# Row-by-row fetch of one subtile in every group of four tiles, shared by SyncE and ScalarE, in a two-layer graph kernel

## The reference

```python
def _L0_gnn_ref(feat, src, dst, W, attn_l, attn_r, bias):
    z = (feat @ W).reshape(N, HEADS, PER_HEAD)
    el = jnp.einsum('nhp,hp->nh', z, attn_l)
    er = jnp.einsum('nhp,hp->nh', z, attn_r)
    e = jax.nn.leaky_relu(el[src] + er[dst], negative_slope=NEG_SLOPE)
    a = jnp.exp(e - emax[dst])
    msg = z[src] * a[:, :, None]
    agg = jax.ops.segment_sum(msg, dst, num_segments=N)
    out = agg / jnp.maximum(denom, 1e-09)[:, :, None]

def _L1_gnn_ref(node_feats, edge_attrs, edge_feats, ...):
    h = jax.nn.silu(edge_feats @ A1 + b1)
    h = jax.nn.silu(h @ A2 + b2)
    tpw = h @ A3
    ss = s[sender]; vs = v[sender]
    # four products of ss, vs, the edge attributes and tpw, summed per receiver, then W_out

h = jnp.maximum(_layernorm(x, axis=-1), 0.0)
x = x + _L0_gnn_ref(h, src, dst, ...)
h = jnp.maximum(_layernorm(x, axis=-1), 0.0)
x = x + _L1_gnn_ref(h, edge_attr_4, edge_attr_8, ...)
```

## Time and profile before

| | us |
|---|---|
| Median of 3 runs | 4041.5 (4036.51 to 4043.6) |
| The profiled execution | 4049.47 |
| Its span, first to last instruction | 4047.6 |
| Mean granted TensorE clock | 0.758 |

### The profile page before, as it was taken

One profiled execution on the slowest core, in us unless ns is written; L12 is line 12 of the kernel. 1 busy time (PEld: TensorE's weight loads), 2 busy tenths in 40 slices (PEclk: granted clock), 3 DMA queues, 4 the chain that ended last, 5 costly groups with the idle time before them and its releaser, 6 DMA issues.

```text
span 4047.6 us, 71477 instructions
## 1 busy us (share of the span) xinstructions
PE 3048.9 (75%) x15640; PEld 2582.1 (64%) x15641; DVE 1948.5 (48%) x4563; ACT 1119.0 (28%) x1869; POOL 2961.1 (73%) x3121
## 2 busy tenths in 40 slices
PE   2566666666667656766659989888899898899898
PEld 2556665566667555665647767666677676676676
DVE  7434434333433433434345555555555555555554
ACT  2334434333433434333331111111111111111111
POOL 1777777777777777777747777777777777777775
PEclk9666666666655665666669888888988989988888
DMA  3434343443434343444422222222222222222221
GB/s 107 119 108 119 111 121 109 124 114 108 119 109 118 112 121 104 124 113 114 118 52 59 59 62 61 60 61 60 59 60 61 61 60 61 60 60 61 60 62 49
DMA packets 208656, 352.07 MB, mean 87 GB/s; under 512 B 99631, under 2 KB 129638, under 8 KB 208326
## 3 DMA queue, kind: packets, MB, share of 16 engines
q0 software_dynamic: 99328, 216.34, 21.3%
q1 hardware_dynamic: 108548, 130.56, 10.4%
q10 hardware_dynamic: 450, 2.44, 0.2%
HBM read 338.22 MB, written 10.85 MB: 86 GB/s over the span
## 4 chain that ended last, share of the span: by engine, by line
POOL 66%; issue 24%; DVE 2%; DMA 2%; PE 2%; POOLq 1%; DVEq 1%; SPq 1%; ACT 1%; ACTq 0%
POOL rows L534 66%; DMA rows<-z_tab,idx 1%; DMA rows<-up_tab,idx 1%; POOLq L280 1%; PE pair L1175 0%; SPq L333 0%; ACT L633 0%; POOLq L281 0%; DVE share L1036 0%; PE pair L1307 0%; DMA win_dram<-share 0%; DVE share L1128 0%; PE pair L1264 0%; DVEq L965 0%; PE pair L1270 0%
## 5 line engine op out<-in xcount | busy, mean ns | idle before, releaser
L534 POOL DMA_INDIRECT rows<-z_tab,idx x1552 | 1477.2, 952 | 554.6 <-issue 546.1
L534 POOL DMA_INDIRECT rows<-up_tab,idx x1552 | 1468.0, 946 | 510.3 <-issue 505.4
L1211 PE MATMUL pair<-acc 128*128 x3168 | 572.1, 327 | 443.3 <-ACT acc L621 441.0
L1211 PEld LDWEIGHTS pair<-acc 128*128 128x128 f32 x3168 | 555.3, 272 | 490.4 <-issue 490.4
L1307 PE MATMUL pair<-share 128*128 128x144 f32 x3136 | 833.8, 354 | 0.0
L1305 PEld LDWEIGHTS pair<-share 128*128 128x128 f32 x3136 | 577.1, 217 | 395.6 <-DVE share L1131 220.4
L1243 PE MATMUL pair<-share,acc 128*128 128x136 f32 x3136 | 676.6, 400 | 0.3
L1305 PE MATMUL pair<-share 128*128 128x48 f32 x3136 | 573.1, 268 | 101.3 <-DVE share L1131 101.1
L1243 PEld LDWEIGHTS pair<-share,acc 128*128 128x128 f32 x3136 | 639.2, 299 | 0.5 <-issue 0.4
L1128 DVE TENSOR_TENSOR share<-rows,pair 128x384 f32<-128x384 f32 x784 | 396.6, 547 | 412.7 <-DMA rows<-up_tab,idx 397.6
L1307 PEld LDWEIGHTS pair<-share 128*128 128x128 f32 x3136 | 544.7, 217 | 0.0
(11 more groups left out here) (172 smaller groups left out, 1890.2 us busy)
## 6 DMA issues: line engine op xcount, KB each, us to landing
acc<-dst_tab SPq DMA_DIRECT2D x198, 512.0 KB
lent<-z_tab SPq DMA_DIRECT2D x2060, 0.6 KB
lent<-up_tab SPq DMA_DIRECT2D x2060, 0.5 KB
rows<-z_tab,idx POOLq DMA_INDIRECT x1552
rows<-up_tab,idx POOLq DMA_INDIRECT x1552
ef_sb<-in_edge_f SPq DMA_DIRECT2D x198, 32.0 KB
z_tab<-rows SPq DMA_DIRECT2D x7, 504.0 KB, 3.2
y_sb<-in_edge_y SPq DMA_DIRECT2D x198, 16.0 KB
```

The lines of the kernel that those rows point to most:

```text
L534: pool.indirect_dma_start(out=rows[:, s, t, 0:width], out_offset=None, in_=table, in_offset=bass.IndirectOffsetOnAxis(ap=indices[:, t:t + ...
L1211: mm = t.matmul(bank[6 + h][:, i * 16:i * 16 + 16], hotT[:, h, i * P:(i + 1) * P], er_flat[:, bass.ds(at, 1), :].rearrange("p a f -> p (a ...
```

## The change

**Fetch.** The eighth subtile of the fourth tile is now taken from POOL in every group, not in every third. Its 128 rows are split: SP fetches 80 rows, 20 in each tile, and ACT fetches 48, 12 in each tile. The buffer `lent` becomes two, used in turn, with semaphores of their own for SP's and ACT's rows. SP reads a list of 128 offsets once per group. ACT fetches its parts 2 and 3 of this group's buffer in tiles 0 and 1, and parts 0 and 1 of the next group's in tiles 2 and 3; SP fetches parts 1 to 3 of this group's buffer in tiles 0 to 2, and part 0 of the next one's in tile 3. ACT copies the buffer in the third tile of every group. POOL issues 31 gathers in every group: 1519 per layer.

**Loops.** SP's and ACT's loop bodies hold two groups (`pairs`) where they held three; POOL's and DVE's hold one.

**Blocks.** DVE centres the block and copies the transposed block out of PSUM itself; ACT only takes the square root (`std_block`). SP stores a group's finished blocks one group later than before.

The diff, cut to its core:

```diff
-PER = 3
-LENT = GI // PER
-PARTS = (12,) * 8 + (8,) * 4
+SP_PARTS = (20, 20, 20, 20)
+ACT_PARTS = (12, 12, 12, 12)
+SP_ROWS, ACT_ROWS = sum(SP_PARTS), sum(ACT_PARTS)
...
-        lent = sb("lent", [P, ZW])
-        lent_idx = sb("lent_idx", [1, 2 * P], I32)
+        lent = sb("lent", [P, 2, ZW])
+        lent_idx = sb("lent_idx", [1, 2, P], I32)
...
-        def thirds(eng, body):
-            with eng.Fori(0, LENT) as r:
-                for e in range(PER):
-                    body(r, e)
-            for e in range(GI % PER):
-                body(LENT, e)
+        def pairs(eng, body):
+            with eng.Fori(0, GI // 2) as i:
+                for e in range(2):
+                    body(i * 2 + e, i, e)
+            body(GI - 1, GI // 2, 0)
+
+        def fetch(eng, kind, landed, first, sizes, i, buf, table, width):
+            at, size = first + sum(sizes[:i]), sizes[i]
+            _, offsets = nc.values_load_multi_w_load_instructions(
+                lent_idx[0:1, buf, at:at + size], engines=(kind,), min_val=0, max_val=(NODES - 1) * width,
...
+            for j, offset in enumerate(offsets):
+                eng.dma_start(lent[at + j:at + j + 1, buf, 0:width // 4].bitcast(U8),
+                              table[bass.ds(offset, width)].rearrange("(a b) -> a b", a=1)).then_inc(landed[buf], 16)
...
+            def first_rows(s_l, n, k, table, width):
+                hold(sp, s_l["copied"], k * GI + 1)
                 load_list(s_l, n, 0, 0)
+                hold(sp, s_l["list"], k * (16 * GI) + 16)
+                sp_rows(s_l, 0, 0, table, width)
+
+            def rows_ahead(s_l, n, k, q, e, s, table, width):
+                last = isinstance(q, int)
+                if s == 1 and not last:
+                    hold(sp, s_l["copied"], k * GI + q + 1)
+                    load_list(s_l, n, q + 1, 1 - e)
+                if s < U - 1:
+                    sp_rows(s_l, s + 1, e, table, width)
+                elif not last:
+                    hold(sp, s_l["list"], (k * GI + q) * 16 + 32)
+                    sp_rows(s_l, 0, 1 - e, table, width)
...
                         load_targets(s, q * U + (s + AHEAD))
+                        rows_ahead(s_l1, 0, k, q, e, s, z_bytes, 4 * ZW)
                         if s == 2:
-                            blocks(sp, q + 1, store_up)
-                        fetch_ahead(s_l1, 0, k, r, e, s, z_bytes, 4 * ZW)
+                            blocks(sp, q, store_up)
...
-                            gather(s, idx[:, s, :], tab, width, s_l["rows"][s],
-                                   T - 1 if e == PER - 1 and s == U - 1 else T)
+                            gather(s, idx[:, s, :], tab, width, s_l["rows"][s], T - 1 if s == U - 1 else T)
...
+            def rows_ahead(s_l, k, q, e, s, table, width):
+                if s < 2:
+                    act_rows(s_l, s + 2, e, table, width)
+                elif not isinstance(q, int):
+                    if s == 2:
+                        hold(act, s_l["list"], (k * GI + q) * 16 + 32)
+                        hold(act, s_l["copied"], k * GI + q + 1)
+                    act_rows(s_l, s - 2, 1 - e, table, width)
...
-                nc.scalar.activation(rows[:, U - 1, T - 1, 0:width], lent[:, 0:width], ACT.Copy)\
+                act.wait_ge(s_l["sp_rows"][e], before * (16 * SP_ROWS) + 16 * SP_ROWS)
+                act.wait_ge(s_l["act_rows"][e], before * (16 * ACT_ROWS) + 16 * ACT_ROWS)
+                nc.scalar.activation(rows[:, U - 1, T - 1, 0:width], lent[:, e, 0:width], ACT.Copy)\
...
-                v.tensor_scalar(nmr1, mv1[:, 0:1], -1.0, None, ALU.mult).then_inc(s_mid["mean"], 1)
-                dve.wait_ge(s_mid["norm"], b + 1)
+                v.tensor_scalar(hc_sb, xs, mv1[:, 0:1], 0.0, ALU.subtract, ALU.max).then_inc(s_mid["centred"], 1)
+                dve.wait_ge(s_mid["turned"], b + 1)
+                v.tensor_copy(hcT_sb, bank[0][:, 0:P]).then_inc(s_mid["turned_sb"], 1)
+                dve.wait_ge(s_mid["std"], b + 1)
```

More of the change, by code:

```diff
@@ L49 @@
 LW = ZW + HEADS
[L50 to L56 removed]
+SP_PARTS = (20, 20, 20, 20)
+ACT_PARTS = (12, 12, 12, 12)
+SP_ROWS, ACT_ROWS = sum(SP_PARTS), sum(ACT_PARTS)
+assert SP_ROWS + ACT_ROWS == P and len(SP_PARTS) == len(ACT_PARTS) == U and GI < P and GI % 2 == 1
 assert NB == BU * BI and NG == U * GI and NG * GE >= EDGES and PAD_DST >= NODES + 3 * P and WIN + HALF - 1 <= P
@@ L256, in gnn_kernel @@
         s_in = named("in", node_steps)
-        s_mid = named("mid", ("mean", "centred", "norm", "turned", "turned_sb", "lin", "row", "stored"))
+        s_mid = named("mid", ("mean", "centred", "std", "turned", "turned_sb", "lin", "row", "stored"))
         s_out = named("out", ("agg_staged", "agg", "added", "stored"))
         def edge_sems(tag, names):
-            return named(tag, ("added", "open", "list", "landed", "copied") + names) \
-                | {n: sems(f"{tag}_{n}_slot", U) for n in ("rows", "in")}
+            return named(tag, ("added", "open", "list", "copied") + names) \
+                | {n: sems(f"{tag}_{n}_slot", U) for n in ("rows", "in")} \
+                | {n: sems(f"{tag}_{n}_buf", 2) for n in ("sp_rows", "act_rows")}
         idx_set = sem("idx_set")
@@ L296, in last_blocks, with rows_landed @@
                 work(b)
[L298 to L302, removed]
-        def thirds(eng, body):
-            with eng.Fori(0, LENT) as r:
-                for e in range(PER):
-                    body(r, e)
-            for e in range(GI % PER):
-                body(LENT, e)
+        def rows_landed(s, q):
+            return q * (16 * (T - 1)) + 16 * (T - 1) if s == U - 1 else q * (16 * T) + 16 * T
+        def pairs(eng, body):
[7 more added lines that the diff above has]
+                lent_idx[0:1, buf, at:at + size], engines=(kind,), min_val=0, max_val=(NODES - 1) * width,
+                skip_runtime_bounds_check_because="they are byte offsets of source nodes, which are rows of the table")
+            for j, offset in enumerate(offsets):
+                eng.dma_start(lent[at + j:at + j + 1, buf, 0:width // 4].bitcast(U8),
+                              table[bass.ds(offset, width)].rearrange("(a b) -> a b", a=1)).then_inc(landed[buf], 16)
+        z_bytes = z_tab.rearrange("n f -> (n f)").bitcast(U8)
+        up_bytes = up_tab.rearrange("n f -> (n f)").bitcast(U8)
         IN1 = 16 * (NG + AHEAD) // 2
@@ L409, in store_up @@
                   .then_inc(s_mid["stored"], 16)
[L411 to L442, removed]
@@ L444, in fetch_first, with sp_rows, load_list @@
-            def fetch_first(s_l, n, k, table, width):
-                load_list(s_l, n, 0, 0)
-                hold(sp, s_l["list"], k * (16 * (LENT + 1)) + 16)
-                hold(sp, s_l["copied"], k * LENT + 1)
-                fetch(s_l, 0, 0, table, width)
+            def sp_rows(s_l, i, buf, table, width):
+                fetch(sp, mybir.EngineType.SP, s_l["sp_rows"], 0, SP_PARTS, i, buf, table, width)
+            def load_list(s_l, n, r, buf):
+                sp.dma_start(lent_idx[0:1, buf, :], lent_dram[n:n + 1, bass.ds(r * P, P)]).then_inc(s_l["list"], 16)
```

116 lines of the change are left out of this document (55 added, 61 removed).

## The result

| | us | ratio to before |
|---|---|---|
| Before, median of 4 runs on the same chip | 4039.15 (4036.51 to 4043.6) | |
| Changed, median of 4 runs | 4211.81 (4206.13 to 4219.21) | 1.0425, 95% interval 1.0407 to 1.0443 |
| Its profiled execution, and its span | 4206.13, 4204.3 | |

What follows compares the result with a forecast made beforehand. POOL's gathers bound the kernel before; SP was to take over at 40.25 and 42.3 us per group, ending layer 2 167 us later: 4049.5 + 167 = 4217 profiled, less 8 gives 4209 us; own range 4110 to 4330, overall 3955 to 4330.

Steps and rivals of the forecast that it cites:

- POOL sets the pace before; 31 gathers are 38.8 us: Both layers: before, each lasts as long as POOL's 1552 gathers; afterwards 31 at 1.251 us make 38.8 us per group.
- SP's sum: SP's rows, register loads, stores, list and loop return: 40.25 us per group in layer 1, 42.3 in layer 2.
- The Trainium skill's price for register loads: SP's loads: about 200 ns per register would make 20 values 1.6 us dearer than 12; the trace's line gave 0.45.
- The extrapolation from 8 and 12: SP's register load: 0.692 us for 8 values and 0.919 for 12, extended by line to 1.37 for 20.
- The end of layer 1, 40 us later: Layer 1: SP's last row issued at 2088 against POOL's last gather end at 2048.2, so the layer ends 40 us later.
- The hindrance of the two sequencers: Rival: SP and ACT hinder each other, or ACT binds; rows at 0.368 us, 298 us more, 4507 us; chance 0.13.
- ACT at 35.4 us per group, no bound: ACT with 48 added rows takes about 35.4 us per group, below POOL; binds only if a row costs over 0.4.
- The rival "ACT binds": ACT's added row fetches set the pace if a row costs it over 0.4 us; chance 0.13, shared with sequencers hindering each other.
- Centring on DVE, at nothing, at worst 20 us of cost: Block centring moved to DVE: nothing on the path; with the cover gone at most 49 x 0.4 = 20 us.
- SP keeps up: Rival: POOL still sets the pace and the whole 82.6 us gain comes, 3959 us; chance 0.18.
- How lateness reaches POOL: Third and fourth tiles: ACT's copy waits for SP's last 20 rows, DVE's fourth tile for the copy, POOL for DVE.

Runs made afterwards that it cites:

- f1: Changed kernel with SP fetching 60 rows per group (parts 16, 16, 16, 12), ACT still 48, 20 rows left out: 4135.58 us, 1.0216 of before.
- f3: Changed kernel with SP at 60 rows (16, 16, 16, 12) and ACT at 28 (8, 8, 8, 4), 40 left out: 4033.57 us, 0.9964 of before.
- e2: Changed kernel with ACT fetching 7 rows per tile instead of 12, SP still 80 per group, 20 left out: 4178.0 us, 1.034 of before.
- f2: Changed kernel with ACT fetching 28 rows per group (8, 8, 8, 4), SP still 80, 20 left out: 4178.1 us, 1.0317 of before.
- f4: Changed kernel with ACT again centring the blocks and copying the transposed block, as before the change: 4251.68 us, 1.0505 of before.
- e3: Changed kernel with all 128 rows fetched, 18 per tile on SP and 14 on ACT: 4842.63 us, 1.1994 of before.
- e1: Changed kernel with SP fetching 15 rows per tile instead of 20, ACT still 12, 20 rows left out: 4176.85 us, 1.0332 of before.
- e4: Changed kernel with all 128 rows fetched, 16 per tile on SP and 16 on ACT: 4560.54 us, 1.1305 of before.
- h1: Kernel before plus new scheme in layer 1 alone, four-group loop bodies, SP's stores every second group; slower session: 5889.62 us, 1.0398 of before.

## Why the prediction was right, step by step

- **POOL sets the pace before; 31 gathers are 38.8 us.** Right. Wherever nothing else held layer 1 (f1, f3), the group took 38.9.
- **SP's sum.** Right, and nearly term by term. By SP's own loads the group of layer 1 lasts 39.97 us (40.25 predicted), that of layer 2 42.3 (42.3). Rows follow each other at 0.334 and 0.331 us (0.33), the load of 20 values is 1.39 (1.37), the way back in the loop 2.72 us (2.7). SP's rows ran in layer 2 from 2110.1 to 4176.4, 2066.3 us; the prediction had them from 2128.3 to 4194, 2066. That layer 2 fits so well is in part luck: with ACT relieved SP's group there is 41.9 (e2, f2), so SP's own sum was 0.4 too long, and the chain of ACT and PE gave that back.
- **The Trainium skill's price for register loads.** The row of the trace decided rightly for 20 values: 1.39 us and not 1.6 us more than for 12. The extrapolation from 8 and 12 held because the pieces of 20, like those of 8 and 12, start at multiples of four values; the prediction names no such condition. Where they don't, 7, 14, 15 and 18 values take about 1.7, 3.1, 3.3 and 3.9 us. The Trainium skill (Runtime: NRT & Kernel Launch, Instruction fetch mechanics) puts a register at about 200 ns even in bulk, and these loads agree with it, at 0.20 to 0.25 us per value; those that start at a multiple of four don't, with 0.057 us for each further value.
- **The end of layer 1, 40 us later.** Too late by 18: SP's first row of layer 2 was issued at 2110.0, not at 2128.3. 48 groups x 0.28 us are 13 of it. The profiled execution was thus 157 us longer than before (4206.1 against 4049.5), not 167. That the median came out within 3 us of 4209 owes something to chance: the 8 us by which the median of before lies under its profiled execution were taken off again, while here the median lies 6 us above it.
- **The hindrance of the two sequencers.** Not seen. Rows on SP cost 0.33 us with ACT fetching 12 rows per tile (changed kernel), and SP's group of layer 1 is 39.9 with 12 rows on ACT and with 7 or 8.
- **ACT at 35.4 us per group, no bound.** This is the term that was wrong, without cost to the number. Its rows cost what was said (0.343 us, load 0.94). What was left out is that ACT's rows stand between two products of PE in layer 2, so that the chain PE, ACT, PE gets longer by each of them. The sum was made for layer 1 alone, and in layer 2 the chain is about 42.1 us (f1), as long as SP's. In layer 1 f4 shows that little was left as well. The prediction came out right since SP's 42.3 lay on top of both. The rival "ACT binds" was given its chance on the price of a row, which was fine; its real ground, the place of the rows between PE's products, wasn't named, and a forecast by the prediction's own sum (the full 38.8 in both layers, 3957 us) was 179 us wrong for f1 and 77 for f3.
- **Centring on DVE, at nothing, at worst 20 us of cost.** Undoing it costs 32 to 40 us (f4), so it was no cost: it keeps ACT under SP in layer 1. How much of that is the work and how much ACT's longer way back isn't shown.
- **SP keeps up.** Fell: SP has no slack left in the trace, and nor would the 3959 us have come if it had kept up (f1, f3).
- **How lateness reaches POOL.** The prediction named ACT's copy of the late rows and DVE's fourth tile. ACT's copy waited for row fetches only 36.2 us in 24 places, and POOL waits most for ACT's indices, 211.6 us. DVE's wait for the copy was there, 90.8 us in layer 1 and 34.4 in layer 2, 1.3 us per group over both, and small beside its 667.9 us for ACT's exponentials. ACT's and SP's programs as a whole run late; the copy is one gate among others.

## What to carry to other kernels

Before work moves onto a sequencer, add up all that it issues per round and compare that with the round of the engine that is relieved; here the sum from five rows of the trace hit the round within 1%, and SP's waits before the change (13.5 us per group in layer 1, 9.2 in layer 2) told at once that 37 more rows at 0.33 us, 12.3 us, wouldn't fit in layer 2 and would leave next to nothing in layer 1. Do the same sum for each layer, and for the second engine ask not only how long its work is but between which two steps of another engine's chain it will stand. Work that is taken off a bound is worth only what the next chain lets through: the whole 0.9 us per group in layer 1 once SP was relieved (f1), and nothing in layer 2, even with both relieved (f3). Look at the parts of a median, too: the 2.7 us of e3's load is a time that no load took.

## What the runs showed of the hardware that was not expected

- **A register load is quick where it starts at a multiple of four values.** There, loads of 8, 12, 16 and 20 values take 0.69, 0.92, 1.17 and 1.39 us in the median, 0.057 per value. Elsewhere 15 values take 3.1 to 3.4 us (e1), 18 take 3.7 to 4.0 and 14 take 3.0 to 3.3 (e3). A count that is no multiple of four costs less: the first piece of layer 1's lists, at 0, takes 1.40 us with 15 values (e1) and 0.99 with 16 (e4).
- **The way back to a loop's start depends on the body.** In layer 1 ACT's took 0.27 us with 317 instructions in the body, 3.3 with 325 (f4), 2.6 with 349 (e3) and 2.9 with 381 (e4), in the median; SP's took 2.7 with 417 and 2.8 with 439 (changed kernel). Length alone isn't the rule: ACT's body of 367 instructions in layer 2 (e4) took 0.23. Where the body lies may count; that wasn't tested.
- **Rows one by one became far dearer in the slower session.** The same train of 20 rows took 6.4 us in the changed kernel and up to 20.3 in h1.
